# Spreading the output units over slots 4 to 7 of a cross-attention decoder layer, with residual rows in three homes

## The chip, the cores and the metric

The kernel runs on one core of a Trainium2 chip. The core has five engines that run their own instruction queues and meet at semaphores: PE (TensorE, matrix products), DVE (VectorE), ACT (ScalarE), POOL (GpSimd) and SP (SyncE, which only issues DMAs here; ACT issues some too). The metric is the device time of one execution in microseconds (us). Results in PSUM are reached by PE, DVE and ACT.

## What is computed

A decoder layer over 16 sequences of 256 tokens and width 512 (16 heads of 32), and a non-local block behind it, all in f32:

```
def attention(q, k, v, mask):
    scores = jnp.einsum('bhqd,bhkd->bhqk', q, k) / jnp.sqrt(jnp.float32(HD))
    scores = scores * mask - 10000.0 * (1.0 - mask)
    probs = jax.nn.softmax(scores, axis=-1)
    return jnp.einsum('bhqk,bhkd->bhqd', probs, v)
ln_out = layernorm(hidden_states, ln1_s, ln1_b)
q, k, v = jnp.split(ln_out @ w_qkv + b_qkv, 3, axis=-1)
x = hidden_states + merge_heads(attention(...)) @ w_ao + b_ao          # self-attention
q = layernorm(x, ln2_s, ln2_b) @ w_q + b_q
k, v = jnp.split(encoder_states @ w_kv + b_kv, 2, axis=-1)
x = x + merge_heads(attention(...)) @ w_co + b_co                      # cross-attention
x = x + gelu(layernorm(x, ln3_s, ln3_b) @ w1 + b1) @ w2 + b2
...
return wy + x                                                          # non-local block
```

## The kernel before

Every f32 operand of a product is split into a high and a low part (tiles that end in `_h` and `_l`), and a product is three matrix products, at lines 66, 67 and 68.

The attention part is 16 **bodies**: bodies 0 to 7 are self-attention, bodies 8 to 15 cross-attention, each over two sequences (512 tokens, four row tiles of 128). A body `k` has eight **slots** `h`. In each slot PE works on three stages of a pipeline at once: it turns the exponentials of one group of four heads (line 1071), weighs the values with them (line 1089), makes the scores of a later group (line 1055), and makes two **units** of 12 products each, which `units_at` names: a query unit `q` and a key unit `k` in slots 0 to 3, and value units `v` and output units `o` in slots 4 to 7. The output units belong to the body before (`k - 1`). All units, and the weighing, take turns in two PSUM banks (the tile `banks`), three turns in a slot. So the first unit of a slot waits until the second unit of the slot before has been read out, and the second unit waits until the weighed values of the slot before have been scaled (line 1694).

Who reads a unit out: ACT writes the high part of a `q` or `k` unit (lines 1295 and 1299), DVE then the low part (line 1639, after it waited for the high one). A `v` unit is read by ACT alone (line 1301), an `o` unit by DVE alone, which adds the residual row tile (line 1634). POOL has added the output bias to that row tile before (`add_bias`, line 779); SP stores the sum (`store`), ACT loads the rows (`load_res`). The residual rows live in `res`, which has two places, so row tiles 2 and 3 are loaded when 0 and 1 have been stored.

The order of all work is written out by hand: each engine has a function `slot(...)` that runs through one slot. DVE's order in a slot is: first half of the masking (line 1656, reads the scores `sc`, waits for PE's turning), the reciprocals (1673, 1676), in slot 2 `aggregate` (1611), scaling (1694), a block transpose of one head's exponentials (1686), four maxima (1666), the second half of the masking (1656), the first unit's read-out, four maxima, then what is attached to the slot, then the second unit's read-out. Attached are: in slots 0 and 1 two row statistics each (`row_statistics`, line 1604), in slots 3 and 4 two block transposes of normalised rows each (line 1814), in slots 6 and 7 one low half of the turned rows each (`lower_pair`, line 1623). ACT's order is: two exponentials (1309), two copies of turned exponentials (1368), the bias and high part of the weighed values (1375, 1378), an exponential, a copy, the first unit, five exponentials, in slots 6 and 7 an `upper_pair` after the second of them, and the second unit. Loads are hooked behind single exponentials by `loads(k, r, h, n)`, where `n` is the exponential's number, 0 to 7. POOL starts a slot's work with a wait for the slot's last maxima (`until_maxima`), then makes the low part of the weighed values (line 820).

DMAs of SP that matter here: in each slot it loads the transposed exponentials (`load_exponentials`), stores the softmax inverses, stores the exponentials in blocks (four DMAs), and reads the inverses back broadcast (`A_rt<-inverses`, four DMAs), in this order in one queue; line 1694 waits for the last of them. In slot 5 it also loads a pair of turned rows and row tile 0 and stores output row tiles 0 and 1, in slot 7 it stores 2 and 3.

Body 7 also splits the cross-attention's weights (16 `chunks` of 256 KB: SP loads them into the four places of `wst`, ACT makes the high part, DVE (line 1580) or POOL (line 831) the low one, in the slots that `chunk_at` names).

The MLP and the non-local block follow from 1246 us on in nested loops, which the change leaves as they are but for semaphore counts.

## Time and profile before

| | |
|---|---|
| median of 3 runs | 2008.2 us (2006.98 to 2008.48) |
| profiled execution, its own time | 2011.13 us |
| its span, first to last instruction | 2009.3 us |
| PE busy | 1976.2 us (98%) |
| DVE busy | 1470.8 us (73%) |
| ACT busy | 1162.6 us (58%) |
| POOL busy | 550.2 us (27%) |
| granted TensorE clock, mean | 0.999 |

Busy time counts every instruction on its engine, waits left out; a matrix product's end is modelled. The profiled execution took 2.9 us more than the median of the runs. The attention's bodies 1 to 14 lie between 138.69 and 1159.26 us of the span, about half of it.

### The profile page before, as it was taken

The page shows a single profiled execution, that of the slowest core. Times are in us where ns is not written, and L with a number is a line of the kernel's source. Part 1 is how long each engine was busy: PE and PEld are TensorE (multiplying, and loading weights), DVE is VectorE, ACT ScalarE, POOL GpSimd, SP SyncE. Part 2 cuts the span into 40 slices and gives each one's busy share as a digit, 9 for nine tenths or more (in the row PEclk, how much of TensorE's full clock was granted, in tenths as well). Part 3 has the DMA queues.
Part 4 walks back from the last instruction along what each step waited for, and adds up shares of the span by engine and source line. Part 5 has one row for each costly group of instructions (what it writes and reads, how often), then busy time and mean ns, then how long its engine had stood idle before and what let it go on. Part 6 is the DMA issues. An engine that isn't in the chain of part 4 may idle for free. (4 is left out here: it accounts for less than half of the span.)

```text
span 2009.3 us, 41550 instructions
## 1 busy us (share of the span) xinstructions
PE 1976.2 (98%) x13632; PEld 1570.0 (78%) x13632; DVE 1470.8 (73%) x3868; ACT 1162.6 (58%) x3251; POOL 550.2 (27%) x556
## 2 busy tenths in 40 slices
PE   9999999999999999999999998999999999999998
PEld 8877777777776777777777776888888888888887
DVE  7799999999999999899899888564444343435333
ACT  4388878888888888888888788421111121212111
POOL 1012222222224344323423432053132131313000
PEclk9999999999999999999999999999999999999999
DMA  8546667567668867767767734531212212121201
GB/s 279 168 94 139 146 165 155 128 168 161 135 173 193 195 172 173 168 162 180 176 152 183 170 90 116 171 107 35 79 42 68 68 47 78 47 63 52 61 24 48
DMA packets 681720, 252.67 MB, mean 126 GB/s; under 512 B 533312, under 2 KB 626112, under 8 KB 681536
## 3 DMA queue, kind: packets, MB, share of 16 engines
q1 hardware_dynamic: 535616, 195.84, 38.5%
q10 hardware_dynamic: 145920, 54.55, 11.2%
q8 instruction: 95, 1.56, 0.3%
q14 instruction: 89, 0.73, 0.1%
HBM read 167.41 MB, written 82.84 MB: 125 GB/s over the span
## 5 line engine op out<-in xcount | busy, mean ns | idle before, releaser
L1309 ACT ACTIVATE A_p<-A_p,A_nmax 128x256 f32<-128x256 f32 x1024 | 507.1, 500 | 5.4 <-DVE A_res L1634 1.7
L1666 DVE CUSTOM_DVE_ANT_0 A_p<-A_p,A_ma 128x256 f32<-128x256 f32 x1024 | 376.6, 423 | 4.6
L1656 DVE TENSOR_TENSOR A_p<-A_sc,A_mk 128x1024 f32<-128x1024 f32 x256 | 312.3, 1220 | 48.0 <-PE A_tp L1071 47.4
L820 POOL TENSOR_TENSOR A_ct_l<-A_cx,A_ct_h 128x256 fp32r<-128x256 f32 x122 | 114.3, 937 | 652.3 <-DVE A_nmax L1666 639.1
L1368 ACT ACTIVATE A_pt<-A_tp 128x512 f32<-128x512 f32 x396 | 218.5, 588 | 47.2 <-PE A_tp L1071 45.9
L1071 PEld LDWEIGHTS A_tp<-A_ident,A_p 128*128 128x128 f32 x1584 | 178.8, 141 | 71.2 <-ACT A_p L1309 33.0
L1071 PE MATMUL A_tp<-A_ident,A_p 128*128 128x128 f32 x1584 | 222.5, 277 | 1.5 <-DVE A_xt_l L1617 0.7
L1505 ACT ACTIVATE A_mk<-A_tp,A_cols 128x512 f32<-128x512 f32 x62 | 42.8, 690 | 269.1 <-PE A_tp L68 269.0
L1309 ACT ACTIVATION_READ_ACCUMULATOR A_p<-A_p,A_nmax 128x1 f32 x1024 | 197.2, 193 | 0.0
L1505 ACT ACTIVATE A_ma<-A_tp,A_cols 128x512 f32<-128x512 f32 x62 | 42.8, 690 | 242.5 <-PE A_tp L68 242.5
L66 PE MATMUL A_banks<-A_xt_h,A_w_h 128*128 128x512 f32 x384 | 162.2, 422 | 3.4 <-DVE A_res L1634 2.1
L929 POOL TENSOR_TENSOR A_v<-A_v,A_b_row 128x512 f32<-128x512 f32 x32 | 52.7, 1664 | 362.3 <-DMA A_v<-x 362.3
L68 PE MATMUL A_banks<-A_xt_h,A_w_l 128*128 128x512 f32 x384 | 151.1, 394 | 0.0
L67 PE MATMUL A_banks<-A_xt_l,A_w_h 128*128 128x512 f32 x384 | 150.1, 391 | 0.0
L1857 DVE CAST A_h_h<-A_ma 128x512 fp32r<-128x512 f32 x64 | 30.5, 476 | 160.4 <-ACT A_ma L1505 156.7
L1375 ACT ACTIVATE A_cx<-A_cx,A_bias_sum 128x256 f32<-128x256 f32 x128 | 65.2, 510 | 139.8 <-DVE A_cx L1694 139.7
L66 PE MATMUL A_tp<-A_xt_h,A_w_h 128*128 128x512 f32 x368 | 143.4, 390 | 0.2 <-DVE A_xt_l L1871 0.2
L67 PE MATMUL A_tp<-A_xt_l,A_w_h 128*128 128x512 f32 x368 | 143.2, 389 | 0.0
L68 PE MATMUL A_tp<-A_xt_h,A_w_l 128*128 128x512 f32 x368 | 143.2, 389 | 0.0
L1089 PE MATMUL A_banks<-A_pt,A_v 128*32 128x256 f32 x2048 | 137.9, 387 | 4.8 <-DMA A_pt<-exponentials 2.1
L1857 DVE CAST A_h_h<-A_mk 128x512 fp32r<-128x512 f32 x64 | 29.1, 454 | 143.6 <-ACT A_mk L1505 141.5
L66 PE MATMUL A_banks<-A_w_h,A_ct_h 128*128 128x512 f32 x256 | 105.7, 413 | 1.6 <-issue 1.1
(248 smaller groups left out, 5001.7 us busy)
## 6 DMA issues: line engine op xcount, KB each, us to landing
exponentials<-A_ln_shift SPq DMA_DIRECT2D x464, 64.0 KB, 2.7
A_pt<-exponentials SPq DMA_DIRECT2D x116, 256.0 KB, 3.1
A_rt<-inverses SPq DMA_DIRECT2D x512, 32.0 KB, 2.4
x<-A_res SPq DMA_DIRECT2D x64, 256.0 KB, 3.6
A_res<-x ACTq DMA_DIRECT2D x58, 256.0 KB, 4.1
turned<-A_x ACTq DMA_DIRECT2D x224, 64.0 KB, 2.8
A_x<-x SPq DMA_DIRECT2D x54, 256.0 KB, 3.7
A_x<-x ACTq DMA_DIRECT2D x42, 256.0 KB, 3.1
```

What stands on the lines that cost most here:

```text
L66: pe.matmul(out, sh, mh, start=first, stop=False)
L67: pe.matmul(out, sh, ml, start=False, stop=False)
L68: return pe.matmul(out, sl, mh, start=False, stop=last)
L820: pool.tensor_tensor(ct_l[:, f, part], cx[:, :], f32(ct_h[:, f, part]), ALU.subtract).then_inc(c_lo, 1)
L1071: last = pe.transpose(tp[:, n % 2, c * S + t * P:c * S + (t + 1) * P], p[:, g % 2, j, t, c * P:(c + 1) * P], ident[:, :])
L1089: last = pe.matmul(banks[rr, bank, 0:S], v[:, b * TPB + c, f * P + j * HD:f * P + (j + 1) * HD], turned_keys(grp, j, c), start=(c == 0), s ...
L1309: act.activation(p[:, g % 2, j, t, :], p[:, g % 2, j, t, :], ACT.Exp, scale=-1.0, bias=nmax[:, g % 2, j, t:t + 1], accum_out=rsum[:, g % 2 ...
L1368: act.activation(pt[:, moved(grp) + i, :, :], tp[:, n % 2, :].rearrange("p (c s) -> p c s", c=TPB), ACT.Copy)\
L1375: act.activation(cx[:, :], cx[:, :], ACT.Identity, bias=bias_sum[:, layer(k, h, -2), 2, f:f + 1]).then_inc(c_sum, 1)
L1505: act.activation(hf[f % 4], hidden_bank(blk, f), ACT.Gelu_apprx_tanh, bias=b1_col[:, f:f + 1])\
L1656: dve.tensor_tensor(p[:, g % 2, heads, :, :].rearrange("p j t s -> p j (t s)"), sc[:, heads, :], m, ALU.mult)\
L1666: dve.tensor_tensor_reduce(out=a_, in0=a_, in1=ma[:, b, t, :], scale=-1.0, scalar=BIG, op0=ALU.add, op1=ALU.min, accum_out=nmax[:, g % 2, ...
```

## The change

- `units_at`: slots 4 to 7 had (v0, v1), (o0, o1), (v2, v3), (o2, o3); now they have (o0, v0), (v1, o1), (o2, v2), (v3, o3), so each has one unit that DVE reads and one that ACT reads.
- Residual row tile 0 (and 3, except in the last body) now lives in the second half of `o_bias` in bodies 0 to 7 and in `wst` in bodies 8 to 15, with semaphores `ld_ends` and `st_ends` of its own; tiles 1 and 2 keep the two places of `res`. The second output bias is loaded in body 9. `add_bias` moves to slots 3, 4, 5 and 6, one each (body 1: 1, 1, 5, 6; bodies 7 and 15: three in slot 1, one in slot 6). SP stores tile 0 in slot 4, tile 1 in slot 6, tiles 2 and 3 in slot 7.
- DVE: in slots 0 and 1 the second unit's low half (the keys') comes before the two row statistics; in slots 3 and 4 one and two of the row transposes come after the second unit.
- ACT: the loads of rows, context, masks and residual rows move behind the slot's last exponential (`n` = 7), and most of them to another slot.
- POOL: the split of context row tiles 2 and 3 is in slot 7 whole; it was spread over slots 6 and 7.
- Body 7: the weight chunks' splits are (0, 1), (2, 3), (4, 5), (6, 7) in slots 4 to 7 instead of (0, 1, 2), (3), (4, 5), (6, 7), and the loads of chunks 4 and 5 move from SP's queue in slot 5 to ACT's. In body 1 the output weights are split in slots 0, 1 and 2 instead of 2, 3 and 4.

```diff
-        chunk_at = {(7, 4): (0, 1, 2), (7, 5): (3,), (7, 6): (4, 5), (7, 7): (6, 7)}
+        chunk_at = {(7, 4): (0, 1), (7, 5): (2, 3), (7, 6): (4, 5), (7, 7): (6, 7)}
...
-            return [(("q", h), ("k", h)), (("v", 0), ("v", 1)), (("o", 0), ("o", 1)), (("v", 2), ("v", 3)),
-                    (("o", 2), ("o", 3))][max(0, h - KT + 1)]
+            return [(("q", h), ("k", h)), (("o", 0), ("v", 0)), (("v", 1), ("o", 1)), (("o", 2), ("v", 2)),
+                    (("v", 3), ("o", 3))][max(0, h - KT + 1)]
...
-        O_SPLITS = {2: (0,), 3: (1,), 4: (2, 3)}
+        O_SPLITS = {0: (0,), 1: (1,), 2: (2, 3)}
...
+        def res_tile(k, t):
+
+            if ends(k, t):
+                return o_bias[:, 1, :] if k < NB else wst[:, 0, :]
+            return res[:, t % 2, :]
...
+        def adds_at(k, h):
+
+            if k == 0:
+                return ()
+            if k == NU:
+                return {1: (0, 1, 2), 4: (3,)}.get(h, ())
+            if k == 1 or k in EARLY_ADDS:
+                return {1: (0, 1) if k == 1 else (0, 1, 2), 5: (2,) if k == 1 else (), 6: (3,)}.get(h, ())
+            return {3: (0,), 4: (1,), 5: (2,), 6: (3,)}.get(h, ())
...
-                if h == (5 if k < NU else 3) and k:
-                    for t in range(2):
+                if k:
+                    for t in ({3: (0, 1), 5: (2, 3)} if k == NU else {4: (0,), 6: (1,), 7: (2, 3)}).get(h, ()):
                         store(k - 1, r - 1, t)
...
-                if by_blocks(k - 1) and (h, n) in ((0, 3), (0, 4), (1, 3)):
-                    load_row(k + 1, r + 1, 2 * h + n - 2)
-                if NB <= k + 1 < NU and n == 4 and h in (1, 2):
+                if by_blocks(k) and (h, n) in ((6, 7), (7, 7)):
+                    load_row(k + 2, r + 2, h - 5)
+                if by_blocks(k - 1) and (h, n) == (0, 7):
+                    load_row(k + 1, r + 1, 3)
+                if NB <= k + 1 < NU and n == 7 and h in (1, 2):
                     load_context(r + 1, h - 1)
...
-                if 1 < k < NU and h == (2 if k < NU - 1 else 0) and n in (5, 6):
-                    load_res(k - 1, r - 1, n - 5)
-                if 0 < k < NU and h == 6 and n in (5, 6):
-                    load_res(k - 1, r - 1, n - 3)
+                if 0 < k < NU:
+                    early_ = {(0, 6): 0, (0, 7): 1, (1, 0): 2, (5, 7): 3}
+                    t = (early_ if k in EARLY_ADDS else {(0, 7): 0, (3, 7): 1, (4, 7): 2, (5, 7): 3}).get((h, n))
...
-                if by_blocks(k) and h in (3, 4) or k == NU - 1 and 3 <= h < 3 + TT:
-                    for t in (2 * h - 6, 2 * h - 5) if by_blocks(k) else (h - 3,):
-                        dve.wait_ge(ln_x, (r + 1) * TT + (t + 1))
-                        dve.transpose(x[:, t, :], x[:, t, :]).then_inc(a_blk, 1)
-                if k < NU and h in ((0, 1) if k else (1, 2)):
-                    row_statistics(r + 1, 0 if h == (0 if k else 1) else 2)
-                    row_statistics(r + 1, 1 if h == (0 if k else 1) else 3)
+                if by_blocks(k) and h == 3 or k == NU - 1 and 3 <= h < 3 + TT:
+                    row_blocks(r, h - 3)
...
                 unit_out(b_, r, k)
                 if k == 1 and h in O_SPLITS:
                     split_raw(3, O_SPLITS[h])
+                if 0 < k < NU and h in (0, 1):
+                    row_statistics(r + 1, 2 * h)
+                    row_statistics(r + 1, 2 * h + 1)
+                if by_blocks(k) and h in (3, 4):
+                    for t in (1,) if h == 3 else (2, 3):
+                        row_blocks(r, t)
```

Left out are the definitions of `ends`, `res_loaded`, `res_free`, `res_stored`, `load_chunk` and `row_blocks`, the semaphore counts that follow from them, and POOL's lines, whose effect the rows below show.

DVE's order in slot 1 of body 5, from the last maxima of the slot to the scaling in slot 2 (`A_p<-A_sc` is the masking, `A_k_l` the keys' low half, `A_stats` the row statistics). Before:

```order
L1666 ISA A_p,A_nmax<-A_p,A_ma 128x256
L1666 ISA A_nmax 128x1
L1604 BN_STATS A_stats<-A_x 128x6 x2
L1639 SCALAR_TENSOR_TENSOR A_k_l<-A_banks,A_bias_sum,A_k_h 128x512
L1656 TENSOR_TENSOR A_p<-A_sc,A_mk 128x1024
L1673 RECIPROCAL A_rinv<-A_rsum 128x8
L1676 STREAM_TRANSPOSE A_turned_inv<-A_rinv 128x32
L1611 BN_AGGR A_mv<-A_stats 128x2 x4
L1694 TENSOR_TENSOR A_cx<-A_banks,A_rt 128x256
```

And of the changed kernel, the same place:

```order
L1708 ISA A_nmax 128x1
L1681 SCALAR_TENSOR_TENSOR A_k_l<-A_banks,A_bias_sum,A_k_h 128x512
L1646 BN_STATS A_stats<-A_x 128x6 x2
L1698 TENSOR_TENSOR A_p<-A_sc,A_mk 128x1024
L1715 RECIPROCAL A_rinv<-A_rsum 128x8
L1718 STREAM_TRANSPOSE A_turned_inv<-A_rinv 128x32
L1653 BN_AGGR A_mv<-A_stats 128x2 x4
L1736 TENSOR_TENSOR A_cx<-A_banks,A_rt 128x256
```

The keys' low half and the two statistics have changed places; nothing else in the slot has.

POOL's order in slots 5 to 7 of a cross-attention body (`A_ct_l` the weighed values' low part, one a slot; `A_et_h` and `A_et_l` the two steps of a context row tile's split; `A_o_bias` is read by the bias adds). Before:

```order
L820 TENSOR_TENSOR A_ct_l<-A_cx,A_ct_h 128x256
L808 CAST A_et_h<-A_e 128x4x128
L813 TENSOR_TENSOR A_et_l<-A_e,A_et_h 128x4x128
L808 CAST A_et_h<-A_e 128x4x128
L813 TENSOR_TENSOR A_et_l<-A_e,A_et_h 128x4x128
L808 CAST A_et_h<-A_e 128x4x128
L820 TENSOR_TENSOR A_ct_l<-A_cx,A_ct_h 128x256
L813 TENSOR_TENSOR A_et_l<-A_e,A_et_h 128x4x128
L779 TENSOR_TENSOR A_res<-A_res,A_o_bias 128x512 x2
L808 CAST A_et_h<-A_e 128x4x128
L820 TENSOR_TENSOR A_ct_l<-A_cx,A_ct_h 128x256
L813 TENSOR_TENSOR A_et_l<-A_e,A_et_h 128x4x128
```

And now:

```order
L851 TENSOR_TENSOR A_ct_l<-A_cx,A_ct_h 128x256
L814 TENSOR_TENSOR A_res<-A_res,A_o_bias 128x512
L839 CAST A_et_h<-A_e 128x4x128
L844 TENSOR_TENSOR A_et_l<-A_e,A_et_h 128x4x128
L839 CAST A_et_h<-A_e 128x4x128
L844 TENSOR_TENSOR A_et_l<-A_e,A_et_h 128x4x128
L851 TENSOR_TENSOR A_ct_l<-A_cx,A_ct_h 128x256
L814 TENSOR_TENSOR A_wst<-A_wst,A_o_bias 128x512
L839 CAST A_et_h<-A_e 128x4x128
L851 TENSOR_TENSOR A_ct_l<-A_cx,A_ct_h 128x256
L844 TENSOR_TENSOR A_et_l<-A_e,A_et_h 128x4x128
L839 CAST A_et_h<-A_e 128x4x128
```

A bias add stands in slot 5, ahead of the split of context tiles 0 and 1; in slot 6 only a bias add is left beside `A_ct_l`; and after slot 7's `A_ct_l` come three steps of the context split (the last, another line 844, follows this piece) where one came before.

## Rows read from the trace of the kernel before

**Rows 1.** The page: busy time by engine.
```profile
PE 1976.2 (98%) x13632; PEld 1570.0 (78%) x13632; DVE 1470.8 (73%) x3868; ACT 1162.6 (58%) x3251; POOL 550.2 (27%) x556
```

**Rows 2.** Windows of bodies 5, 7, 11, sum of fourteen: length, busy us, clock.
```profile
429.83:501.57 71.74, 71.53 (x609) 54.80 (x608) 66.23 (x203) 59.92 (x183) 17.19 (x19) 1.00 0.66 149
...
573.33:649.68 76.35, 72.58 (x609) 54.86 (x609) 70.19 (x204) 63.31 (x187) 31.09 (x31) 1.00 0.74 184
...
868.13:941.31 73.18, 71.88 (x609) 54.83 (x608) 66.71 (x203) 59.69 (x184) 25.87 (x29) 1.00 0.72 169
...
sum 1020.57, PE 1006.22 PEld 767.86 DVE 943.34 ACT 846.90 POOL 327.38; mean PE 71.87 PEld 54.85 DVE 67.38 ACT 60.49 POOL 23.38
```

**Rows 3.** PE timeline (start us, length, operation), body 5: scores, slots 4, 5.
```profile
465.98 0.39 PE L1055 MATMUL A_sc<-A_k_h,A_q_h 32*128 32x256 f32 x4
...
474.88 0.39 PE L1055 MATMUL A_sc<-A_k_h,A_q_h 32*128 32x256 f32 x4
```

**Rows 4.** DVE timeline, body 5: masking after slot 4's scores; idle before.
```profile
468.68 1.22 DVE L1656 TENSOR_TENSOR A_p<-A_sc,A_mk 128x1024 f32<-128x1024 f32 x1 [1.08 <-PE A_tp L1071]
```

**Rows 5.** DVE timeline, body 5, end of slot 3; then PE.
```profile
457.83 1.30 DVE L1814 STREAM_TRANSPOSE A_x<-A_x 128x512 f32<-128x512 f32 x2
459.05 0.71 DVE L1639 SCALAR_TENSOR_TENSOR A_k_l<-A_banks,A_bias_sum,A_k_h 128x512 fp32r<-128x512 f32 x1
...
459.82 0.50 PE L66 MATMUL A_banks<-A_w_h,A_xt_h 128*128 128x512 f32 x1 [0.20 <-DVE A_k_l L1639]
```

**Rows 6.** Body 11, slots 2 to 4: a load, a scaling, PE's wait.
```profile
884.56 0.39 ACTq L1331 DMA_DIRECT2D A_res<-x  x1
...
891.31 0.42 DVE L1694 TENSOR_TENSOR A_cx<-A_banks,A_rt 128x256 f32<-128x256 f32 x1 [0.96 <-DMA A_rt<-inverses]
...
898.79 0.50 PE L66 MATMUL A_banks<-A_w_h,A_et_h 128*128 128x512 f32 x1 [0.79 <-DVE A_k_l L1639]
```

**Rows 7.** PE timeline, body 11: the wait after slot 7.
```profile
935.15 0.50 PE L66 MATMUL A_banks<-A_xt_h,A_w_h 128*128 128x512 f32 x1 [0.49 <-DVE A_res L1634]
```

**Rows 8.** Body 7: DVE's weight split in slot 4, PE's waits after it.
```profile
611.29 3.07 DVE L1580 SCALAR_TENSOR_TENSOR A_w_l<-A_wst,A_lns_q,A_w_h 128x512 fp32r<-128x512 f32 x2
...
620.07 0.39 PE L1055 MATMUL A_sc<-A_k_h,A_q_h 32*128 32x256 f32 x4 [0.73 <-DVE A_p L1656]
631.81 0.42 PE L1089 MATMUL A_banks<-A_pt,A_v 128*32 128x256 f32 x4 [1.86 <-DMA A_pt<-exponentials]
```

**Rows 9.** DVE timeline, body 5, slot 1: scaling, statistics, keys' low half.
```profile
434.10 0.42 DVE L1694 TENSOR_TENSOR A_cx<-A_banks,A_rt 128x256 f32<-128x256 f32 x1
...
439.59 1.28 DVE L1604 BATCH_NORM_STATS2 A_stats<-A_x 128x6 f32<-128x512 f32 x2
440.79 0.73 DVE L1639 SCALAR_TENSOR_TENSOR A_k_l<-A_banks,A_bias_sum,A_k_h 128x512 fp32r<-128x512 f32 x1
```

**Rows 10.** ACT timeline, body 5, slot 1: keys' high half.
```profile
439.42 0.67 ACT L1299 ACTIVATE A_k_h<-A_banks,A_bias_sum 128x512 fp32r<-128x512 f32 x1
```

**Rows 11.** DVE timeline, body 5, slot 2: scaling, masking, keys' low half.
```profile
443.37 0.39 DVE L1694 TENSOR_TENSOR A_cx<-A_banks,A_rt 128x256 f32<-128x256 f32 x1
...
445.65 1.22 DVE L1656 TENSOR_TENSOR A_p<-A_sc,A_mk 128x1024 f32<-128x1024 f32 x1
...
449.38 0.75 DVE L1639 SCALAR_TENSOR_TENSOR A_k_l<-A_banks,A_bias_sum,A_k_h 128x512 fp32r<-128x512 f32 x1 [0.47 <-ACT A_k_h L1299]
```

**Rows 12.** Body 2, slot 2: DVE's second masking, PE's scores after it.
```profile
229.57 1.22 DVE L1656 TENSOR_TENSOR A_p<-A_sc,A_mk 128x1024 f32<-128x1024 f32 x1
...
230.94 0.39 PE L1055 MATMUL A_sc<-A_k_h,A_q_h 32*128 32x256 f32 x4 [0.18 <-DVE A_p L1656]
```

**Rows 13.** Timelines of POOL and DVE, body 11: a cast, two maxima.
```profile
931.41 0.62 POOL L808 CAST A_et_h<-A_e 128x512 fp32r<-128x512 f32 x1
...
931.69 0.62 DVE L1666 CUSTOM_DVE_ANT_0 A_p<-A_p,A_ma 128x256 f32<-128x256 f32 x1
...
932.24 0.41 DVE L1666 CUSTOM_DVE_ANT_0 A_p<-A_p,A_ma 128x256 f32<-128x256 f32 x1
```

More of the change, by code:

```diff
@@ L616, in step @@
                     sp.dma_start(mk[:, 0, :, :], xm_d[0]).then_inc(ld_m[0], DMA)
-                    for c in range(2):
-                        sp.dma_start(o_bias[:, c, :], across(out_biases[c])).then_inc(ld_o, DMA)
+                    sp.dma_start(o_bias[:, 0, :], across(out_biases[0])).then_inc(ld_o, DMA)
                 if n >= 3:
@@ L630, in slot @@
                     load_inverses(r, h)
+                if (k, h) == (NB + 1, 1):
+                    sp.wait_ge(st_ends, 2 * NB * DMA)
+                    sp.dma_start(o_bias[:, 1, :], across(out_biases[1])).then_inc(ld_o, DMA)
                 if h == 0 and k == NU:
-                    for t in range(2):
+                    for t in range(3):
                         load_res(k - 1, r - 1, t)
                 if h == 4 and k == NU:
-                    for t in range(2):
-                        load_res(k - 1, r - 1, t + 2)
+                    load_res(k - 1, r - 1, 3)
                 if k == 0 and h == 0:
@@ L879, in slot @@
                     addend(1, r - (NB - 2))
-                if h == (4 if 1 < k < NU - 1 else 1) and k:
-                    add_bias(k - 1, r - 1, 0)
-                    add_bias(k - 1, r - 1, 1)
+                if h != 3:
+                    for t in adds_at(k, h):
+                        add_bias(k - 1, r - 1, t)
                 if k == NB - 1 and 2 <= h < 2 + TT:
@@ L905, in slot @@
                     normalise(r + 1, 1 if h in (2, 5) else 3)
+                if h == 3:
+                    for t in adds_at(k, h):
+                        add_bias(k - 1, r - 1, t)
                 if h == 2:
@@ L1329, in load_res, with load_chunk @@
             def load_res(k, r, t):
[L1330 to L1331 removed]
+                wait(act, *res_free(k, t))
+                if (k, t) == (NB, 0):
+                    act.wait_ge(w_lo2, sum(1 for c_, _ in chunks[:13] if c_))
+                act.dma_start(res_tile(k, t), row_tile(0, k, r, t)).then_inc(res_loaded(k, t)[0], DMA)
             def load_o_copy(t):
                 act.dma_start(turned_w[KT + t], fold_wt[3][t * P:(t + 1) * P, :]).then_inc(ld_tw[t], DMA)
[L1336 to L1340 removed]
+            def load_chunk(n):
+                c, t = chunks[n]
+                if chunks[n - KT][0] == 0:
+                    act.wait_ge(w_lo, 4 * KT + chunks[n - KT][1] + 1)
+                else:
+                    act.wait_ge(w_lo2, sum(1 for c_, _ in chunks[:n - KT + 1] if c_))
+                act.dma_start(wst[:, n % KT, :], x_weights[c][t * P:(t + 1) * P, :]).then_inc(ld_s[n % KT], DMA)
```

80 lines of the change are left out of this document (44 added, 36 removed).

## The prediction

> **What bounds the kernel now.** I read the page's busy times first. PE is busy in 98% of the span, DVE in 73%, ACT and POOL in less [rows 1]. A change that touches no matrix product can give back only what PE sits idle. The second view is the table of windows, a row for each of bodies 1 to 14 [rows 2]; the third is PE's timeline from one slot's scores to the next slot's. In a slot where nothing comes late, scores start 474.88 - 465.98 = 8.90 us apart [rows 3], so a body's floor is 8 x 8.90 = 71.20 us. The fourteen bodies take 1020.57 us [rows 2], 14 x 71.20 is 996.8, and the difference of **23.8 us** is all that this change can win there. The rows show how uneven it is: body 5 is 0.5 over the floor, body 11 is 2.0, body 7 is 5.15 [rows 2].
>
> The fourth view is who ended PE's idle times. Three kinds of place hold most of the 23.8:
> - *After slot 3*, the first unit waits for the keys' low half, which DVE writes behind two row transposes of 1.30 us: 0.20 us idle in body 5 [rows 5], 0.79 in body 11, where the scaling of slot 3 had waited 0.96 for the inverses' DMA, with residual loads issued 7 us before [rows 6]. Over fourteen bodies I count 8.9 us.
> - *After slot 7*, the first unit waits for output unit 3's read-out: 0.49 in body 11 [rows 7]; 5.6 us in all.
> - *Body 7's slots 4 to 6*: DVE splits two weight chunks in one go of 3.07 us, then PE's scores wait 0.73 for the masking; later the weighing waits 1.86 for a DMA of exponentials [rows 8]. I put 3.5 us on these.
> The rest, 5.8, is spread (bodies 1 and 2 hold 2.0 of it).
>
> DVE's time in a slot is counted from the start of the scores, F. The next slot's masking cannot start before F+2.70, since it waits for PE's turning [rows 4]. PE wants to start the next first unit at about F+2.75, and starts it 0.06 after the low half's end (459.05+0.71, then 459.82) [rows 5]: a read-out that ends by F+2.69 costs nothing.
>
> **The change part by part.**
>
> *Keys' halves ahead of the statistics (slots 0 and 1).* Before, DVE runs the two statistics (1.28 us as shown, 1.20 from start to next start) and then the keys' low half, 439.59 to 441.5 [rows 9]. The statistics fill the time in which ACT still writes the high half: it lasts 0.67 from 439.42, thus to 440.09 [rows 10], 0.50 after 439.59. Now DVE waits out that 0.50 in each of the two slots and runs the statistics behind the low half. The sum of DVE's work in such a slot was exactly full (low half's end 441.52, masking at once), so it falls behind: 0.52 at slot 1's masking, 1.04 at slot 2's, counting from F+2.70. Slot 1's second masking has room. In slot 2 aggregation comes first, and the second masking stood at 445.65, 2.28 after the scaling [rows 11]. Late by 1.04 it starts at F+7.88; scores start 1.37 after it begins (230.94 - 229.57 [rows 12]), at F+9.25 where 8.90 is free: **0.35 lost**. The keys' high half follows the scaling by 440.09 - 434.10 = 5.99 [rows 9, 10] and in slot 2 was already awaited (DVE idle 0.47 before 449.38 [rows 11]); with the scaling 1.04 late the low half ends at 3.08 of the new F instead of 2.69: **0.39 lost**. That is 0.74, I take **0.75 us a body**. Bounds: nothing, if ACT's high half comes earlier in the new order; 1.0 if nothing is absorbed.
>
> *Slots 3 and 4.* One of slot 3's transposes moves behind the low half, which then ends near F+2.1, inside 2.69 also if it starts with the 0.29 that is left over. The 8.9 us go. What is late next is the masking behind the moved transpose: 2.11+0.65 = 2.76 against 2.70, nothing. In slot 4 output unit 0 is read first, and both transposes end near 4 with slack taken from maxima: nothing.
>
> *One output unit a slot.* Slot 7 now reads one output unit on DVE and one value unit on ACT; output unit 3 ends near F+2.3. The 5.6 us go. In slots 4 and 6 the value unit is second and DVE is free of it. POOL makes output unit 2's operand in slot 5, at F+1.4 to 2.1, before 2.75. SP's stores of tiles 0, 1 and 2, 3 stand in slots 4, 6, 7; tile 3's wait ends by F+2.3 and holds the exponentials' loads behind it in SP's queue up to then, which is before they are ready anyway. Bias adds, one a slot on POOL, are far shorter than a slot, and POOL is the least busy of the four [rows 1]: hidden.
>
> *Loads behind the last exponential.* They are issued some 0.6 us later than before and in other slots; ACT itself pays nothing. The context's loads and the residual loads no longer share slot 2 in bodies 8 to 14, so the 0.96 wait [rows 6] should shrink; I credit this within the 8.9, and take no more.
>
> *Context split whole in slot 7 (bodies 7 to 13).* POOL gets about 4.1 us of casts and differences in slot 7 instead of half that. Beside a cast of 0.62, a DVE maximum takes 0.62 instead of 0.41 [rows 13]. Four casts slow DVE by up to 0.8 instead of 0.4, in slots with some slack, so between 0 and 1.4; I take **0.3** a body, times seven 2.1.
>
> *Body 7.* Two chunks a slot instead of three cap DVE's block but not the 3.07 itself [rows 8]; splits in slot 5 become two. SP loses two chunk loads, which should free the exponentials behind the 1.86 wait. I leave 2.2 of 5.15 us: between 0.75 and 5.15, nearer the low end because the longest wait is the one that SP's queue bears on.
>
> *Bodies 1 and 2.* The output weights' splits move into slots 0 to 2, where DVE is full: body 1 stays at 2.6 (0.75 to 4), body 2 falls from 2.95 to 1.5. Body 15, outside the fourteen, gains the same reorder once: +0.4. The MLP and what follows are the same.
>
> **Sum.** After: 2.6 + 1.5 (bodies 1, 2), 4 x 0.75 = 3.0 (3 to 6, which had 1.9 and lose 1.1), 2.2 (7), 7 x 1.05 = 7.35 (8 to 14, which had 11.2): 16.65. Saved 23.8 - 16.65 - 0.4 = 6.75. The profiled execution took 2011.13 us, 2.9 more than the median of 2008.2; it would come to 2004.4, and the median to **2001.4**.
>
> **The rivals.**
>
> *A. The gaps cost nothing.* If ACT reaches the keys' high half sooner, because loads left its queue and the second unit's product ends earlier, the 0.75 vanishes. Then bodies 1 to 14 keep perhaps 6 of 23.8: 2008.2 - 18 = 1990. For it: quiet slots show idle DVE time (1.08 before the masking [rows 4]) that could take the work in. Against: slots 0 and 1 have none [rows 9], and the high half's 5.99 behind the scaling is a chain of ACT work that the change leaves. Floor, with nothing left: 2008.2 - 23.8 = 1984.4.
>
> *B. POOL's bunch slows DVE: the slower side.* The last context split is pushed into slot 7, where DVE's low half of rows, output unit 3 and next slot 0's statistics follow closely. By [rows 13] each cast costs 0.21 of a maximum beside it; if its differences cost as much, eight operations cost 1.65 us in slot 7 and slot 0, where DVE has no slack. The seven cross bodies then cost 1.4 more than in the sum, 9.8 in all, and 2001.4 + 9.8 = 2011. It turns slower than before once the bunch adds over 1.0 us of lag a cross body. On POOL's port the Trainium skill's GPSIMD Engine Reference, section "1. Specifications", says that it shares its SBUF interfaces with VectorE, with contention for DVE instructions that have two SBUF inputs; the maxima have two. By that rule all eight operations would slow DVE, and the time would be the 2011 of this rival. The trace shows it for casts; bias adds of POOL beside maxima left those at 0.41, so I see it only in part.
>
> *C. The DMA lateness stays.* The stalls of body 11 begin with inverses that land late [rows 6], and body 7's with exponentials [rows 8]. If the same bytes collide in another slot, the cross bodies keep 0.85 each on top of the reorder's 0.75, and body 7 all of its 5.15: 2.6 + 1.5 + 3.0 + 5.15 + 7 x 1.6 = 23.4, with body 15's 0.4 just 2008. For it: a load moves by only 0.6 us within its slot. Against: the number of loads in a slot does fall.
>
> **How the numbers follow.** Chances: forecast 50%, A 20%, C 20%, B 10%. A run of this kernel can tell about 0.2%, 4 us, from no change. The forecast's own range is 1996 to 2006 (0.75 between 0.3 and 1.0 a body; body 7's and POOL's bounds): nearly all of it is faster. A is faster whole, C lies within 0.2% mostly, B half within and half beyond, and some of each spills: faster 0.72, same 0.15, slower 0.13. The range for 8 in 10 reaches to A and into B: 1989 to 2010.
>
> **What would show it.** In quiet bodies (3 to 6), PE should wait in slot 2 for the second masking (about 0.35) and after it for the keys' low half (about 0.4), with DVE idle 0.5 before the low half in slots 0 and 1 (released by ACT); their length should be 71.9 to 72.0. The waits after slots 3 and 7 should be gone, body 7 near 73.4, cross bodies near 72.3. If slot 2 shows no PE wait, A holds; if inverses or exponentials still end idle times of 0.5 and more, C; if maxima in slot 7 last 0.6 in rows, B. I am wrong altogether if PE waits at a place that before never waited, as for an output unit's operand in slot 6 or residual rows in their new homes.

## The result, and the profile after

| | before | after |
|---|---|---|
| median | 2008.2 us (7 runs) | 2013.4 us (7 runs, 2011.8 to 2017.6) |
| ratio | 1 | 1.0024, interval 1.0014 to 1.0033 |
| profiled execution | 2011.1 us | 2011.8 us |
| the same again, another time | 2009.8 us (22 runs) | 2014.9 us (6 runs), ratio 1.0029, interval 1.0016 to 1.0041 |

The kernel became slower by 5 us, where 2001.4 us and a range of 1989 to 2010 were forecast. The two profiled executions differ by only 0.7 us, so the first trace of before was a long one and the first of after a short one. I took more traces of both for that reason.

The page of after, busy times:

```profile
PE 1977.7 (98%) x13632; PEld 1569.0 (78%) x13632; DVE 1477.9 (74%) x3868; ACT 1161.5 (58%) x3251; POOL 546.5 (27%) x556
```

Beside [rows 1] it shows nothing of use: PE's busy time differs by 0.1%. The windows of after answer to [rows 2] (length; busy time of PE, PEld, DVE, ACT, POOL with counts; clock, DMA share, GB/s), bodies 1, 5, 7, 8, 11 and the sum of bodies 1 to 14:

```profile
138.83:213.83 75.00, 72.70 (x609) 54.77 (x608) 69.60 (x205) 61.38 (x186) 18.51 (x19) 1.00 0.63 141
...
431.53:503.74 72.21, 71.89 (x609) 54.76 (x609) 66.58 (x205) 59.93 (x184) 17.08 (x19) 1.00 0.66 148
...
575.65:650.08 74.43, 72.28 (x609) 54.72 (x609) 69.72 (x204) 62.94 (x187) 30.76 (x31) 1.00 0.76 187
650.08:724.41 74.33, 72.66 (x610) 54.89 (x610) 69.27 (x204) 62.54 (x191) 30.25 (x32) 1.00 0.84 195
...
868.81:941.14 72.33, 71.72 (x609) 54.75 (x609) 67.52 (x203) 59.79 (x183) 25.79 (x29) 1.00 0.73 171
...
sum 1019.14, PE 1007.47 PEld 766.68 DVE 947.59 ACT 846.17 POOL 326.98; mean PE 71.96 PEld 54.76 DVE 67.68 ACT 60.44 POOL 23.36
```

Fourteen bodies stand 1019.14 - 996.8 = 22.3 us over the floor, where I had forecast 16.65. The quiet body 5 takes 0.47 us more than before (72.21 for 71.74). The sums of the second trace of after and of the third of before:

```profile
sum 1021.44, PE 1008.75 PEld 766.70 DVE 946.49 ACT 846.61 POOL 327.39; mean PE 72.05 PEld 54.76 DVE 67.61 ACT 60.47 POOL 23.39
```
```profile
sum 1018.83, PE 1005.77 PEld 767.95 DVE 942.15 ACT 847.37 POOL 327.11; mean PE 71.84 PEld 54.85 DVE 67.30 ACT 60.53 POOL 23.36
```

So before has 23.8, 20.6 and 22.0 us over the floor in three executions, after has 22.3 and 24.6.

**The forecast price is there.** DVE, body 5 of after, slots 1 and 2, then PE (start, length, operation, idle before):

```profile
442.57 0.75 DVE L1681 SCALAR_TENSOR_TENSOR A_k_l<-A_banks,A_bias_sum,A_k_h 128x512 fp32r<-128x512 f32 x1 [0.46 <-ACT A_k_h L1324]
443.24 1.28 DVE L1646 BATCH_NORM_STATS2 A_stats<-A_x 128x6 f32<-128x512 f32 x2
444.43 1.21 DVE L1698 TENSOR_TENSOR A_p<-A_sc,A_mk 128x1024 f32<-128x1024 f32 x1
...
448.55 1.23 DVE L1698 TENSOR_TENSOR A_p<-A_sc,A_mk 128x1024 f32<-128x1024 f32 x1
...
452.26 0.75 DVE L1681 SCALAR_TENSOR_TENSOR A_k_l<-A_banks,A_bias_sum,A_k_h 128x512 fp32r<-128x512 f32 x1 [0.46 <-ACT A_k_h L1324]
```
```profile
449.92 0.39 PE L1080 MATMUL A_sc<-A_k_h,A_q_h 32*128 32x256 f32 x4 [0.18 <-DVE A_p L1698]
...
453.07 0.50 PE L66 MATMUL A_banks<-A_xt_h,A_w_h 128*128 128x512 f32 x1
```

DVE waits 0.46 us for the high half in slot 1, the statistics then push slot 2's masking, and the scores start 1.37 us after the second masking (449.92 - 448.55, as in [rows 12]), 0.59 late here and 0.39 in most bodies; the first unit starts 0.81 - 0.75 = 0.06 after the low half's start and length. From scores to scores, slots 1 and 2 take about 9.28 and 9.31 us in nine of the fourteen bodies of either trace. In some bodies slot 1 takes 9.6 to 9.7: bodies 2, 3 and 8 of the first trace, bodies 2, 8, 9 and 10 of the second. There PE is late twice in slot 1, first for the keys' low half of slot 0 and then for the second masking. Body 8 shows it: the first unit starts 3.16 us after the scores instead of 2.76, and the next scores 9.70 after them:

```profile
659.47 0.39 PE L1080 MATMUL A_sc<-A_k_h,A_q_h 32*128 32x256 f32 x4
...
662.63 0.50 PE L66 MATMUL A_banks<-A_xt_h,A_w_h 128*128 128x512 f32 x1
...
669.17 0.39 PE L1080 MATMUL A_sc<-A_k_h,A_q_h 32*128 32x256 f32 x4 [0.19 <-DVE A_p L1698]
```

**The old waits are gone.** PE's first unit behind slot 3 and behind slot 7 in body 11 of after, where [rows 6] and [rows 7] have 0.79 and 0.49 of idle time (here none is shown):

```profile
899.06 0.48 PE L66 MATMUL A_banks<-A_w_h,A_ct_h 128*128 128x512 f32 x1
```
```profile
935.00 0.48 PE L66 MATMUL A_banks<-A_xt_h,A_w_h 128*128 128x512 f32 x1
```

**A new wait, in slot 5 of bodies 8 to 14.** POOL, then DVE, then PE, body 12 of after:

```profile
991.86 1.29 POOL L844 TENSOR_TENSOR A_et_l<-A_e,A_et_h 128x512 fp32r<-128x512 f32 x1
```
```profile
992.17 1.26 DVE L1708 CUSTOM_DVE_ANT_0 A_p<-A_p,A_ma 128x256 f32<-128x256 f32 x1
993.37 0.41 DVE L1708 CUSTOM_DVE_ANT_0 A_p<-A_p,A_ma 128x256 f32<-128x256 f32 x1
```
```profile
995.76 0.39 PE L1080 MATMUL A_sc<-A_k_h,A_q_h 32*128 32x256 f32 x4 [0.36 <-DVE A_p L1698]
```

The maximum started inside POOL's instruction and ended at 993.43, 0.28 us after POOL's end (993.15). It took 1.26 us instead of 0.41. Slot 5 is too long in all seven bodies, by 0.14 to 0.88 us in the first trace (2.5 us in sum) and by 0.19 to 1.10 in the second (3.6). Before, POOL's step ended just after the maxima began and made the first one some 0.25 us longer, which the slot took up; now a bias add of 1.3 us stands ahead.

Where the time is, us by part, means over three traces of before and two of after, and the change that I had forecast:

| part | before | after | change | forecast |
|---|---|---|---|---|
| up to body 1 | 139.3 | 140.0 | +0.7 | 0 |
| body 1 | 73.8 | 75.0 | +1.25 | 0 |
| body 2 | 73.3 | 73.0 | -0.3 | -1.45 |
| bodies 3 to 6 | 287.1 | 288.4 | +1.3 | +1.1 |
| body 7 | 75.9 | 74.6 | -1.3 | -2.95 |
| bodies 8 to 14 | 508.8 | 509.3 | +0.5 | -3.85 |
| body 15 | 71.8 | 72.8 | +1.0 | +0.4 |
| body 16 | 36.4 | 37.5 | +1.1 | 0 |
| the rest | 741.9 | 741.7 | -0.2 | 0 |
| sum | | | +4.1 | -6.75 |

Body 16 is counted up to its last weighing of values. The same fourteen bodies by slot: us over 8.90 from scores to scores, summed over bodies 1 to 14. The last line is the run `stats_first` of the next section, one trace:

| slot | 0 | 1 | 2 | 3 | 4 | 5 | 6 | 7 | sum |
|---|---|---|---|---|---|---|---|---|---|
| before, mean of three | 1.5 | 1.0 | 0.3 | 8.1 | 2.9 | 0.0 | 3.3 | 5.0 | 22.1 |
| after, mean of two | 1.2 | 8.8 | 6.5 | 1.1 | 0.1 | 4.5 | 0.4 | 1.0 | 23.5 |
| after, order undone | 5.7 | 0.7 | 0.9 | 0.7 | 0.7 | 2.7 | 1.0 | 2.7 | 15.0 |

The change gave back 16.8 us in slots 3, 4, 6 and 7, and took 14.0 in slots 1 and 2 and 4.5 in slot 5.

One more edit is part of the change: in body 9 the splits of the weight chunks 12 to 15 stand in slots 0, 0, 1 and 2 instead of 0, 1, 2 and 3. No run undid it. Slots 0 to 3 of body 9 take 36.4 us in the first trace of after, the same as those of body 10, which has no such split, so it shows no cost there.

### The profile page after: what moved, and what is told of

It reads as the page before. It is cut to its first block and busy times, and to the rows that moved or that the text cites. A ratio compares the mean times of both kernels' runs of the same rounds, so it can differ in the third digit from the quotient of the medians.

```text
span 2010.0 us, 41538 instructions
## 1 busy us (share of the span) xinstructions
PE 1977.7 (98%) x13632; PEld 1569.0 (78%) x13632; DVE 1477.9 (74%) x3868; ACT 1161.5 (58%) x3251; POOL 546.5 (27%) x556
```

## The experiments

**Controls.** The kernel before twice and the changed one once more, without an edit.

> The kernel before, unchanged, for a second trace and as the null of this comparison. Its one trace had lasted 2.9 us longer than the median of its runs, while the changed kernel's trace was 1.6 us shorter than its median, so 4.5 us of the measured difference stand in neither trace. If that is chance between executions (theory D: the waits for DMAs differ from one execution to the next), this trace should show the same waits on the keys' low half and on output unit 3 as the first within 0.2 us each, and differ from it by 1 to 3 us in waits that a DMA ends. If the executions are alike, all waits agree and the two spans differ by less than 1 us. Ratio 1.000 in both cases.

> The kernel before, unchanged, a third trace. The first two held 23.8 and 20.6 us over the floor in bodies 1 to 14, in executions of 2.9 us over and 1 us under the median. If the first was an unlucky one, the third has 20 to 22.5.

> The changed kernel, unchanged, for a second trace. Theory D: slots 0 to 2 repeat (0.4 us lost in slot 1, 0.4 in slot 2), and what differs is waits ended by DMAs, in slots 5 to 7 above all; the span is 1 to 4 us longer than the first one's 2010.0. Rival: the trace repeats within 0.5 us, and the difference of the medians lies in what the profiler's presence changes. Time 2013 in both, 1.002 to 1.003 of the kernel before.

The second trace of before was 2.8 us shorter than the first, the third 0.1 shorter. What differs is single waits in slots 6 and 7 and how late slot 3's inverses are, and also the start: body 1 begins at 138.7 to 141.4 us in the same code, with no difference between kernels that I can show. The guess that the first was an unlucky one was right by about 1.7 us in the bodies, not by more. The waits did not repeat as I had expected: slot 3 holds 8.9, 7.9 and 7.7 us over the floor in the three traces, slot 7 holds 5.6, 4.4 and 5.0. The second trace of after was 4.9 us longer than the first, where I had expected 1 to 4: 2.4 us lie before body 1 and 2.3 in bodies 1 to 14.

**The order of the keys' half and the statistics**, undone in the changed kernel, and alone in the kernel before:

```diff
+                if 0 < k < NU and h in (0, 1):
+                    row_statistics(r + 1, 2 * h)
+                    row_statistics(r + 1, 2 * h + 1)
                 unit_out(b_, r, k)
...
-                if 0 < k < NU and h in (0, 1):
-                    row_statistics(r + 1, 2 * h)
-                    row_statistics(r + 1, 2 * h + 1)
```

> The changed kernel with one thing undone: in slots 0 and 1 DVE runs the two row statistics ahead of the keys' low half, as before. Order theory: the losses of slots 1 and 2 (9.29 and 9.32 us instead of 8.90 in a quiet body, 0.8 a body and more in bodies 1 to 3 and 8) go in fifteen bodies, so 12 us and up to 15 less: 1999 to 2001. Rival (the lag is taken up by slack, or the statistics ahead make slot 3 late again): 4 us less or nothing, 2009 to 2013.

> The kernel before with one thing done: in slots 0 and 1 the keys' low half comes ahead of the two row statistics. Order theory: 0.75 us a body as in the changed kernel, and since slot 3 still has both row transposes ahead of its low half there, the lag is not absorbed and costs 0.2 to 0.3 more: 14 us more, 2022. Rival (what fills slots 1 and 2 in the changed kernel is something else): less than 4 us more, 2008 to 2012.

Undone: 2003.6 us, 11.4 less than the changed kernel on the same chip (0.9972 of before, interval 0.9963 to 0.9981). Alone: 2023.4, 13.5 more than before (1.0072, interval 1.0058 to 1.0085). The second is what I expected (14), the first a little under it (12 to 15). DVE and PE of body 5, slot 1, with the order undone:

```profile
442.40 1.28 DVE L1646 BATCH_NORM_STATS2 A_stats<-A_x 128x6 f32<-128x512 f32 x2
443.60 0.73 DVE L1681 SCALAR_TENSOR_TENSOR A_k_l<-A_banks,A_bias_sum,A_k_h 128x512 fp32r<-128x512 f32 x1
444.35 1.23 DVE L1698 TENSOR_TENSOR A_p<-A_sc,A_mk 128x1024 f32<-128x1024 f32 x1
```
```profile
441.65 0.39 PE L1080 MATMUL A_sc<-A_k_h,A_q_h 32*128 32x256 f32 x4
...
450.55 0.39 PE L1080 MATMUL A_sc<-A_k_h,A_q_h 32*128 32x256 f32 x4
```

No wait for ACT, and 8.90 us from scores to scores. In its place 0.3 to 0.5 us are lost in slot 0 of bodies 4, 5 and 9 to 14; in all, slot 0 holds 5.7 us where it had 1.2, and why was not looked into.

All the other edits together thus bring 2009.84 - 2003.57 = 6.3 us, and I had counted 18 for them. By the table of slots they did give back 14 us in slots 3, 4, 6 and 7; slots 0 and 5 take 7 of that, and bodies 15 and 16 take 1.5. The rest of the experiments look for such losses.

**POOL's steps in slot 5.** First taken away in the changed kernel:

```diff
-            return {3: (0,), 4: (1,), 5: (2,), 6: (3,)}.get(h, ())
+            return {3: (0,), 4: (1, 2), 6: (3,)}.get(h, ())
...
-                    t = (early_ if k in EARLY_ADDS else {(0, 7): 0, (3, 7): 1, (4, 7): 2, (5, 7): 3}).get((h, n))
+                    t = (early_ if k in EARLY_ADDS else {(0, 7): 0, (3, 6): 2, (3, 7): 1, (5, 7): 3}).get((h, n))
```

> The changed kernel, with residual row tile 2 loaded in slot 3 and its bias add made in slot 4 beside tile 1's, so that POOL's context split in slot 5 starts 1.27 us earlier and has ended when DVE's first maxima of the slot begin. Port theory (a DVE instruction with two SBUF inputs that starts during a POOL instruction ends only 0.28 us after it: the maximum at 992.17 of the first trace took 1.26 us instead of 0.41): slot 5 of bodies 8 to 14 goes from 9.04 to 9.78 us down to 8.9 to 9.0, 2.5 us less by the first trace and up to 3.8 by the second: 2010 to 2011 against 2013 to 2015. Rival (slot 5 is long because of late inverses, idle 0.25 to 0.83 us before the scaling): slot 5 keeps 9.1 and more, time the same.

2011.7 us (1.0007, interval 0.9998 to 1.0016). POOL and DVE in body 11:

```profile
918.84 1.29 POOL L844 TENSOR_TENSOR A_et_l<-A_e,A_et_h 128x512 fp32r<-128x512 f32 x1
```
```profile
919.68 0.42 DVE L1736 TENSOR_TENSOR A_cx<-A_banks,A_rt 128x256 f32<-128x256 f32 x1 [0.43 <-DMA A_rt<-inverses]
...
920.64 0.38 DVE L1708 CUSTOM_DVE_ANT_0 A_p<-A_p,A_ma 128x256 f32<-128x256 f32 x1
```

Slot 5 is 8.90 in all seven bodies, also here where the inverses are 0.43 late, so the rival falls. The trace's fourteen bodies are still 22.7 us over the floor, because slot 1 takes 9.55 to 9.70 in bodies 10 and 12 to 14; that the time fell is shown by the medians alone (2011.7 for 2014.9, intervals that just touch). Then put into the kernel before, with nothing else changed:

```diff
                     for t in range(2):
-                        split_context(k + 1, r + 1, t)
+                        upper_context(k + 1, r + 1, t)
+                        if t == 0:
+                            own, part = own_columns(t)
+                            pool.wait_ge(et_hi, (r + 1 - NB) * TT + (t + 1))
+                            pool.tensor_tensor(et_l[:, :, part], own, f32(et_h[:, :, part]), ALU.subtract).then_inc(twice, 1)
+                            pool.wait_ge(twice, r + 1 - NB)
+                        lower_context(k + 1, r + 1, t)
```

> The kernel before with one POOL instruction more: in slot 5 of bodies 8 to 13 the low part of context tile 0 is computed twice, so that tile 1's steps come 1.3 us later, where the changed kernel has them behind its bias add. Nothing else is changed. Port theory: DVE's first maximum of the slot then starts inside tile 1's step and ends 0.28 us behind it, 1.0 to 1.3 us long instead of 0.41, and slot 5 of these bodies goes from 8.90 to 9.0 to 9.4 us: 1 to 3 us in all, ratio 1.0005 to 1.0015. Rival (the long slot 5 of the changed kernel comes from late inverses or from the residual loads in slots 3 to 5): slot 5 stays at 8.90 and maxima at 0.41 to 0.65.

2014.3 us (1.0025, interval 1.0015 to 1.0034). POOL, DVE and PE in body 11:

```profile
920.39 1.36 POOL L814 TENSOR_TENSOR A_et_l<-A_e,A_et_h 128x512 fp32r<-128x512 f32 x1
922.01 0.84 POOL L809 CAST A_et_h<-A_e 128x512 fp32r<-128x512 f32 x1 [0.26 <-ACT A_v L1308]
```
```profile
920.52 1.51 DVE L1673 CUSTOM_DVE_ANT_0 A_p<-A_p,A_ma 128x256 f32<-128x256 f32 x1
921.96 0.41 DVE L1673 CUSTOM_DVE_ANT_0 A_p<-A_p,A_ma 128x256 f32<-128x256 f32 x1
922.31 0.82 DVE L1673 CUSTOM_DVE_ANT_0 A_p<-A_p,A_ma 128x256 f32<-128x256 f32 x1
```
```profile
924.42 0.39 PE L1062 MATMUL A_sc<-A_k_h,A_q_h 32*128 32x256 f32 x4 [0.74 <-DVE A_p L1663]
```

Slot 5 went from 8.90 to between 9.69 and 9.73 us in all seven bodies 8 to 14 (I had written 8 to 13), 5.7 us in sum, twice the upper end of what I expected, since a third maximum meets a cast. One POOL instruction on an engine that is 27% busy cost PE 0.8 us a body.

**Body 1's weight splits** (`O_SPLITS = {2: (0, 1), 3: (2, 3)}` in the changed kernel).

> The changed kernel, with the output weights' splits of body 1 in slots 2 and 3 (two each) instead of slots 0, 1, 2 (one, one, two). Theory: slots 0 and 1 were full once the keys' half had moved, so each split pushed the scaling; in slot 1 it also stood behind POOL's bias add and took 1.52 us instead of 0.6. Slot 1 of body 1 should fall from 11.1 to 9.3, slot 3 rise by up to 0.8: body 1 at 73.9 to 74.3 instead of 75.0, time 1 us less. Rival (body 1's long slot 1 is POOL's bias adds or a DMA and not the splits): body 1 stays at 75.

POOL, DVE and PE of the changed kernel, body 1, slot 1:

```profile
150.64 1.28 POOL L814 TENSOR_TENSOR A_o_bias<-A_o_bias 128x512 f32<-128x512 f32 x1
```
```profile
150.94 1.52 DVE L1616 TENSOR_TENSOR A_w_l<-A_wst,A_w_h 128x512 fp32r<-128x512 f32 x1
```
```profile
155.86 0.50 PE L66 MATMUL A_banks<-A_xt_h,A_w_h 128*128 128x512 f32 x1 [1.31 <-DVE A_cx L1736]
```

Slot 1 fell from 11.14 to 9.29 us, but slot 3 rose from 9.36 to 10.87, so body 1 came to 74.5 instead of 75.0, and the time (2014.4) does not tell the two apart. The splits are shown to be the cause of the long slot 1; moving them moved the loss.

**Body 16's third load** (tile 2's load from slot 0 to 1 of SP, its bias add back to slot 4).

> The changed kernel, with the load of residual row tile 2 in body 16 moved from slot 0 to slot 1 of SP's queue, behind the inverses, and its bias add back to slot 4 beside tile 3's. Queue theory: in the first trace three loads of 256 KB and the turned rows stood ahead of slot 0's store of the inverses, which landed 5.5 us after its issue instead of 3.4, and PE waited 0.5 to 1.5 us for the scaling. Body 16 should fall from 37.5 us to 36.3 to 36.7, the time by 1 us. Rival (the lag comes from the split of the first MLP rows behind three adds on POOL): no less than 37.2 unless POOL's chain ends the wait.

Body 16 took 37.6 us, the time was 2015.9. PE's wait for the scaling in slot 1 went, the length stayed. One thing clouds this trace: TensorE's granted clock was at its lower level for some 6.8 us of body 16 (means of 0.83, 0.50, 0.50, 0.50 and 0.97 in the five windows of 2 us from 1239 to 1249), against some 3.4 us in the traces of after. The time gives no sign of a gain. With the order of the keys' half alone in the kernel before, body 16 takes 36.3 us, so that order is not its cause. Neither theory explains body 16's 1.1 us, and it stays open.

**All four edits together.**

> All four together: statistics ahead of the keys' low half in slots 0 and 1, tile 2's bias add in slot 4, body 1's splits in slots 2 and 3, and body 16's third residual load late. If the parts add up: 2003.6 as with the statistics alone, less 3 for slot 5, 1 for body 1 and 1 for body 16: 1998 to 2000, 0.995 of the kernel before. If they overlap (POOL's steps then meet other maxima), 2001 to 2003.

2001.4 us (0.9954, interval 0.9941 to 0.9968), a little above what I expected of the sum (1998 to 2000); bodies 1 to 14 are 10.6 us over the floor. From this version, four parts were taken back one by one. The intervals of these runs are about 2 to 3 us to either side, so a difference of 1 or 2 us between them is not told from none.

> The version with all four changes, with both row transposes of slots 3 and 4 ahead of the second unit's read-out again. The prediction's term: the low half of slot 3's keys ends behind F+2.69 again, 0.2 to 1.0 us a body, 8.9 us over bodies 1 to 14: 2009 to 2010 against 2001.4. Rival (in this version nothing is late when slot 3 begins, so the transposes only use slack): slot 3 at 8.9 to 9.1, at most 2 us: 2002 to 2003.

Both row transposes ahead of the second unit: 2005.3 us, 3.9 more (4.8 in the trace's bodies, 2.0 of it in body 1). Slot 3 is 9.00 in bodies 9 to 14, where before it was 9.3 to 9.96. So of the 8.9 us that I gave to slot 3, the place of the transposes earned less than half. The rest went with other edits. That a scaling which waited for late inverses had made it in the cross-attention bodies [rows 6] fits the traces, since DVE's waits for inverses between the scores of slots 2 and 3 fell from 4.9, 3.6 and 3.6 us (three traces of before, bodies 1 to 14) to 0.2 and 1.6, but no run shows it by itself.

> The version with all four changes, with the loads that stand behind the slot's last exponential behind an earlier one (n of 3 to 5 as in the kernel before), in the same slots. The prediction took the later issue as worth nothing by itself. Theory: within a slot the place does not matter, 2000 to 2003, no inverses late by more than 0.3 us in slots 3 to 5. Rival (the loads' bytes then stand ahead of the inverses and exponentials): idle times before the scaling of 0.3 to 0.9 us that a DMA of inverses ends return in bodies 8 to 14, 2004 to 2008.

Loads behind exponentials 3 to 5 instead of 7: 2000.0 us, the trace 0.6 us lower. The place within the slot is worth nothing that these runs can tell, as predicted. Moving the loads back to their old slots was not tried.

> The version with all four changes, with body 7's weight chunks split as before (three in slot 4, one in slot 5) and chunks 4 and 5 loaded by SP in slot 5. The prediction gave 2.95 us of body 7's 5.15 to this rearrangement; body 7 took 73.9 us in this version. The prediction's term: body 7 back to 76 or 77 us, slot 4 at 10.5 and slot 6 at 10.8: time 2.5 us more. Rival (body 7's gain came from the units and the statistics, and the rearrangement only moved the long slots to 5, 6 and 7): body 7 at 73.5 to 74.5 us, time the same within 1 us.

Body 7's chunks and their loads as before: 2001.0 us, body 7 at 74.0 against 73.9. The rearrangement brings nothing that can be told: the long slots are 4, 6 and 7 in one and 5, 6 and 7 in the other. In the changed kernel, DVE's block of two chunks stands in slot 5 and the next unit waits for the scaling behind it:

```profile
622.87 2.77 DVE L1622 SCALAR_TENSOR_TENSOR A_w_l<-A_wst,A_lns_q,A_w_h 128x512 fp32r<-128x512 f32 x2 [0.29 <-ACT A_w_h L1298]
```
```profile
627.97 0.51 PE L66 MATMUL A_banks<-A_w_h,A_xt_h 128*128 128x512 f32 x1 [0.78 <-DVE A_cx L1736]
```

> The version with all four changes, with the value and output units of slots 4 to 7 paired again (v0 v1, o0 o1, v2 v3, o2 o3) and SP's stores of tiles 0 and 1 in slot 5, 2 and 3 in slot 7. The prediction's term: the first unit after slot 7 waits for output unit 3's read-out again, 5.6 us over bodies 1 to 14: 2007. Rival (with the bias adds and residual loads spread, output unit 3 is read in time also in pairs, so that the spreading of the units itself brings little): slot 7 within 0.1 us of 8.90 in bodies 3 to 6 and 9 to 13, 2001 to 2003.

> As the pairing of units before (v0 v1, o0 o1, v2 v3, o2 o3), with what made that run useless mended: ACT waited in slot 5 for the store of tile 0, whose place tile 3 takes, and held up its own queue by 4 to 6 us a body; now tile 3 is loaded in slot 6 behind its seventh exponential and its bias is added in slot 7. The prediction's term: the first unit behind slot 7 waits for output unit 3, up to 0.4 us a body, 5.6 us in all: 2005 to 2007 against 2001.4 of the version with all four. Rival (in this version nothing is late in slot 7, the pair is read out in time): 2000 to 2003.

Both of these missed their aim. In the first (2099.9 us) ACT's own queue stood still for 7 us a body, with the load of tile 3 waiting for the store of tile 0 in the place that they share:

```profile
508.10 0.51 ACT L1336 ACTIVATE A_p<-A_p,A_nmax 128x256 f32<-128x256 f32 x1 [7.12 <-DMA x<-A_o_bias]
```

In the second (2039.2 us) the load came in time, but I had put tile 3's bias add behind POOL's wait for slot 7's maxima, and PE waited 2 us for it through output unit 3's read-out:

```profile
504.91 1.26 POOL L816 TENSOR_TENSOR A_o_bias<-A_o_bias 128x512 f32<-128x512 f32 x1
```
```profile
507.02 0.50 PE L66 MATMUL A_banks<-A_xt_h,A_w_h 128*128 128x512 f32 x1 [2.00 <-DVE A_o_bias L1678]
```

What the spreading of the units is worth by itself was not measured. What both runs show is the price of the home that tiles 0 and 3 share: tile 3 can only be loaded when tile 0 has been stored.

> The version with all four changes, with the loads behind earlier exponentials and body 7's chunks as in the kernel before (each alone gave 2000.0 and 2001.0 against 2001.4), and in body 15, slot 5, DVE's split of an MLP chunk behind output unit 1's read-out, where PE waited 0.67. If they add up: body 15's slot 5 from 9.98 to 9.3, 1999 us, ratio 0.994 to 0.995. If not, 2000 to 2001.

2000.2 us (0.9954, interval 0.994 to 0.9967), the same as without the extra edits, though body 15's slot 5 fell from 9.98 to 9.30 as meant. Body 7 took 75.7 us in this one trace, with the chunks as in `chunks_back`, which had 74.0. In the changed kernel that slot looks like this, a split of an MLP chunk ahead of output unit 1's read-out (DVE, then PE):

```profile
1207.18 1.00 DVE L1902 TENSOR_TENSOR A_w_l<-A_e,A_w_h 128x512 fp32r<-128x512 f32 x1 [0.54 <-ACT A_w_h L1541]
1208.11 0.68 DVE L1676 TENSOR_TENSOR A_res<-A_banks,A_res 128x512 f32<-128x512 f32 x1
```
```profile
1208.84 0.50 PE L66 MATMUL A_banks<-A_w_h,A_ct_h 128*128 128x512 f32 x1 [0.42 <-DVE A_res L1676]
```

## Why the prediction was wrong

*Right.* The mechanism of the keys' half ahead of the statistics: its two places stand in slots 1 and 2, 0.38 and 0.41 us in a quiet body for 0.35 and 0.39, and bodies 3 to 6 lost 1.3 for 1.1. Fifteen bodies at 0.75 make 11.25; its removal gave 11.4 and its doing alone cost 13.5. That 11.4 agrees so well is partly luck: by slots, the removal gave back 13.7 us in slots 1 and 2 and lost 4.5 in slot 0. The waits behind slots 3 and 7 are gone: slot 3 went from 8.1 to 1.1 us over the floor, slot 7 from 5.0 to 1.0. The loads' place within the slot is worth nothing that can be told.

*Wrong, by its steps.* The miss is 11 us in the traces (+4.1 for -6.75). No single term made it; these did:

- "Bias adds, one a slot on POOL, ... hidden" failed: not hidden, but 3 us in slot 5 of the cross-attention bodies (2.5 and 3.6), shown by taking the cause away and by dosing it in the kernel before. I had asked only whether POOL has time, and not what POOL's instructions meet on DVE when an add pushes them. Rival B had the mechanism but the wrong slot: I looked at slot 7, where the bunch had been written, and slot 7 stayed at 8.90. Its sentence that bias adds beside maxima left those at 0.41 was wrong too: the adds had lain beside maskings, which read PSUM and kept their 1.22 us. The Trainium skill's GPSIMD Engine Reference, section "1. Specifications", says that contention is for DVE instructions with two SBUF inputs; the trace agrees, with 1.26 us against 0.41. I had that rule before me and gave the rival 10%.
- The forecast was made against one execution's 23.8 us. Three have 22.1 on average: 1.7 us of what was to be won was chance in that trace, in bodies 2 and 8 to 14 above all.
- "Body 7 ... I leave 2.2 of 5.15" failed: 3.2 and 3.5 stayed, and taking the rearrangement back costs nothing that can be told. The body's gain came from other edits.
- Body 1 was held at 2.6 over the floor and has 3.8: a weight split was put behind the keys' half of a full slot and, in slot 1, beside a POOL bias add (1.52 us). The 4 us at the upper end of its bounds was the better guess.
- Body 15 was given 0.4 and cost 1.0: the reorder takes 0.8 us in its slot 2 (10.18 instead of 9.40 us, the same with the order alone), and its slot 5 went from 9.6 to 10.0, since output unit 1 is now read behind an MLP chunk's split.
- "The MLP and what follows are the same": body 16 is 1.1 us longer, cause open.
- The transposes' 8.9 us hold in the sum, since slot 3 did lose its waits, but not in their cause: they were a sum of waits, and the transposes' own place earned 3.9.
- "0.75 us a body" in slots 1 and 2 held only where the slot before was not late. In the others slot 1 pays another 0.3 to 0.4.

*The other rivals.* A (the gaps cost nothing) falls with the two waits of slots 1 and 2. Of C (the DMA lateness stays) the half on lateness came true: over bodies 1 to 14 DVE waited for inverses for 10.0, 7.8 and 8.7 us in the three traces of before and for 9.6 and 14.0 in the two of after, so these waits did not shrink, they moved from slots 2 and 6 to slots 4, 5 and 7 (counted from scores to scores). Its price did not come: slots 3 and 7 are nearly free, and slot 5 is at 8.90 once POOL's steps are early, with late inverses and all. The sign of being wrong altogether, PE waiting where it never had, is slot 5.

Together 1.25 + 1.15 + 0.2 + 1.65 + 4.35 + 0.65 + 1.1 make 10.4 (bodies 1, 2, 3 to 6, 7, 8 to 14, 15 and 16), and 0.7 lies before body 1, where the code is the same and two traces of one kernel differ by up to 2.4. Of the 4.35 in bodies 8 to 14, 0.9 are slot 5's 3.0 against the 2.1 that I had set for slot 7, and 0.8 are the first trace's (11.2, 10.7 and 9.4 us over the floor in three executions of before). The other 2.7 lie in slots 0 to 3, mostly of bodies 8 to 10 (body 8 alone 2.3 us in the first trace of after, 0.75 forecast). Part of them is the order's price again, slot 1's 9.70 for 9.28 us: with the order undone, slots 1 and 2 of bodies 8 to 14 are all at 8.9. Why slot 0 is late in these bodies, no run took apart.

## What to carry to other kernels

An edit that fills DVE's known gap (statistics while ACT still writes) must not be moved without naming what fills the gap next; the waits of a quiet slot could be worked out to 0.05 us from a few rows, but not what they become where the slot before is late. When a POOL instruction is put ahead of others, go through which two-SBUF-input DVE instructions the pushed ones now meet: here one instruction more of 1.3 us, on a POOL that was 27% busy, cost PE 0.8 us a body. Before subtracting from one trace, find how much of its waits another execution of the same kernel has.
